# Recurrent layers: the pieces of one software-pipelined step in a new order on TensorE, ScalarE and VectorE

## What is computed

```python
xa = _ln(x, ln1_w, ln1_b)
sx = concatenate([state[:, 1:2] - xa[:, :1], xa[:, :-1] - xa[:, 1:]], axis=1)
xxx = tanh((xa + sx * maa_x) @ maa_w1).reshape(b, l, 5, DM)
xxx = einsum('blfd,fde->blfe', xxx, maa_w2)
xm = xa[:, :, None] + sx[:, :, None] * (maa_stack + xxx)
xk, xw, xv, xr, xg = (xm[:, :, j] for j in range(5))
w = exp(-exp(time_decay + tanh(xw @ td_w1) @ td_w2))
r, k, v, g = xr @ Wr.T, xk @ Wk.T, xv @ Wv.T, silu(xg @ Wg.T)
# over tokens, per head of 16 channels: out = r (u*k*v + s); s = k*v + w*s
og = group_norm(out) * gn_w + gn_b
x1 = x + og * g @ Wo.T
xc = _ln(x1, ln2_w, ln2_b)             # sx2: the shifted difference of xc
rr = sigmoid((xc + sx2 * ffn_maa_r) @ Wfr.T)
kk = square(relu((xc + sx2 * ffn_maa_k) @ Wfk.T))
return x1 + rr * (kk @ Wfv.T)
```

## Time and profile before

| | us |
|---|---|
| median of 3 runs | 3420.65 |
| lowest, highest | 3415.77, 3423.81 |
| the profiled execution, its own time | 3415.86 |
| its span, first to last instruction | 3414.1 |

### The profile page before, as it was taken

How to read it: one execution, slowest core, us unless ns; L and a number is a source line. 1 busy time by engine, 2 the same in 40 slices (tenths; PEclk the granted TensorE clock), 3 DMA queues, 4 the chain that set the end, 5 groups by cost and what they waited for, 6 DMA issues and landing times.

```text
span 3414.1 us, 77104 instructions
## 1 busy us (share of the span) xinstructions
PE 3145.0 (92%) x32684; PEld 2330.3 (68%) x32684; DVE 2327.4 (68%) x3819; ACT 1822.0 (53%) x3311; POOL 226.0 (7%) x457
## 2 busy tenths in 40 slices
PE   6789999999999999999999999999799899998998
PEld 4567777777777777776777777776566666665666
DVE  3667777777677767768777677776546667566566
ACT  3445555555554555555545555554446656556565
POOL 0000000000000000000000000000011010010110
PEclk8889999999999999999999999999999999999999
DMA  3223322343333233333323333323344224133221
GB/s 124 69 75 107 122 99 99 124 143 115 110 118 105 100 111 127 118 121 118 112 94 115 122 116 108 118 106 140 113 102 96 68 62 115 38 86 103 57 68 51
DMA packets 110357, 349.41 MB, mean 102 GB/s; under 512 B 22848, under 2 KB 56256, under 8 KB 84032
## 3 DMA queue, kind: packets, MB, share of 16 engines
q0 software_dynamic: 39936, 234.91, 21.1%
q1 hardware_dynamic: 69648, 106.28, 9.9%
q10 hardware_dynamic: 432, 3.28, 0.3%
HBM read 252.11 MB, written 16.78 MB: 79 GB/s over the span
## 4 chain that ended last, share of the span: by engine, by line
PE 77%; DVE 12%; ACT 6%; DMA 2%; issue 2%; SPq 1%; DVEq 0%; ACTq 0%
PE psum L742 34%; PE psum L751 6%; PE psum L909 4%; PE psum L927 3%; PE psum L879 3%; PE psum L808 3%; PE psum L869 3%; PE psum L792 3%; PE psum L899 2%; DMA rw<-rw 2%; DVE psum L1718 2%; PE psum L884 2%; ACT rw L1210 2%; PE psum L695 2%; PE psum L675 1%
## 5 line engine op out<-in xcount | busy, mean ns | idle before, releaser
L742 PE MATMUL psum<-rw 128*128 128x256 f32 x6144 | 1461.0, 396 | 73.0 <-DVE rw L1469 63.4
L742 PEld LDWEIGHTS psum<-rw 128*128 128x128 f32 x6144 | 1196.1, 198 | 292.3 <-DVE rw L1469 72.8
L1718 DVE CUSTOM_DVE_ANT_0 psum<-psum,mem 128x1024 f32<-128x1024 f32 x256 | 313.4, 1224 | 76.0 <-PE psum L899 75.8
L1274 ACT ACTIVATE rest<-psum,mem 128x1024 f32<-128x1024 f32 x256 | 284.8, 1113 | 90.4 <-DVE mem L1718 88.5
L909 PE MATMUL psum<-ident,rest 128*128 128x128 f32 x2048 | 269.6, 275 | 2.7 <-DVE mem L1677 1.5
L1514 DVE SCALAR_TENSOR_TENSOR rw<-psum,rw 128x256 f32<-128x256 f32 x480 | 196.1, 475 | 100.3 <-PE psum L708 60.0
L909 PEld LDWEIGHTS psum<-ident,rest 128*128 128x128 f32 x2048 | 234.5, 141 | 42.2 <-issue 14.6
L1143 ACT ACTIVATE rw<-psum 128x512 f32<-128x512 f32 x192 | 113.4, 603 | 272.0 <-PE psum L742 271.7
L1899 POOL DMA_DIRECT2D rw<-big_dram x192 | 101.2, 528 | 2367.7 <-PE psum L742 2333.8
L1186 ACT ACTIVATE rw<-psum,own 128x256 f32<-128x256 f32 x384 | 208.4, 714 | 84.5 <-PE psum L792 84.5
L751 PE MATMUL psum<-rw 128*128 128x512 f32 x432 | 222.1, 633 | 15.0 <-ACT rw L1147 7.9
(11 more groups left out here) (157 smaller groups left out, 4446.3 us busy)
## 6 DMA issues: line engine op xcount, KB each, us to landing
rw<-big_dram POOLq DMA_DIRECT2D x192, 1024.0 KB, 5.1
side<-mem POOLq DMA_DIRECT2D x256, 128.0 KB, 4.1
rw<-xs_dram SPq DMA_DIRECT2D x32, 512.0 KB, 3.4
side<-mem SPq DMA_DIRECT2D x256, 64.0 KB, 2.0
rw<-rw SPq DMA_DIRECT2D x192, 64.0 KB, 2.0
rw<-rw SPq DMA_DIRECT2D x384, 32.0 KB, 3.2
xs_dram<-rw SPq DMA_DIRECT2D x24, 512.0 KB, 2.9
rw<-x_dram SPq DMA_DIRECT2D x16, 512.0 KB, 3.5
```

The lines of the kernel that those rows point to most:

```text
L742: last = mm(t[:, o * TC:(o + 1) * TC], big[:, k, P * m:P * m + P], src[:, k, 0:TC], start=k == 0, stop=k == KT - 1, skip_group_check=True)
L1274: s_ring.empty(f(probs[:, n % HPT, :].rearrange("p (a s) -> p a s", a=2), s_ring.bank(n, "s"), ACT.Exp, scale=-1.0, bias=mx[:, n % 8:n % 8 ...
L1718: maxima.inc(nc.vector.tensor_tensor_reduce(t, t, mbias.rearrange("p (a s) -> p a s", a=2), 1.0, 3.4e38, ALU.add, ALU.min, accum_out=mx[:, ...
```

## The change

The tiles of the attention's first batch, which the last steps carry along (`batch_tile`, `after`, `centred`, `scaled`), are moved among them in the same manner. The core of the diff:

```diff
-C_TILES = [(2, "fr0", "act"), (2, "fr1", "act"), (2, "fk0", "act"), (1, "wo0", "dve"), (1, "wo1", "dve"), (2, "fk1", "act"), (2, "fv0",
-           "dve"), (2, "fv1", "dve"), (1, "s1", "act"), (1, "m1", "dve"), (1, "s2", "act"), (1, "i1", "dve")]
+C_TILES = [(2, "fr0", "act"), (2, "fr1", "act"), (2, "fk0", "act"), (1, "wo0", "dve"), (1, "wo1", "dve"), (2, "fk1", "act"), (1, "s1", "act"), (2, "fv0", "dve"), (2, "fv1", "dve"), (1, "m1", "dve"), (1, "s2", "act"), (1, "i1", "dve")]
...
# VectorE, in norm_c
-                if which == "mix":
+                if which == "mixr":
                     dve.wait_ge(c_dve.sem, c_dve.at(it, "sx"))
                     c_dve.inc(mixture(mixr, sxc, xa_c, lambda k: par(layer, FMR, k)), it, "mixr")
+                if which == "mixk":
+                    dve.wait_ge(c_dve.sem, c_dve.at(it, "sx"))
                     c_dve.inc(mixture(mixk, sxc, xa_c, lambda k: par(layer, FMK, k)), it, "mixk")
...
# VectorE, start of the step
+                if has_e:
+                    norm_c(e, "mixk")
+                if has_c:
+                    gated(c, 1)
                 if has_b:
                     level1(b)
-                    own_values(b)
...
# VectorE, end of the step
-                if has_c:
-                    norm_c(c, "mix")
-                if has_b:
-                    gated(b, 0)
-                    gated(b, 1)
+                if has_b:
+                    group_variance(b, 1)
                 if s == ITS - 1:
                     after(0, "q0")
                     scaled(0, 0)
+                if has_b:
+                    group_scale(b, 1)
+                if s == ITS - 1:
                     scaled(0, 1)
+                if has_b:
+                    gated(b, 0)
```

More of the change, by code:

```diff
@@ L113 @@
-B_TILES = [("P0a", "dve"), ("P0b", "dve"), ("P1", "dve"), ("P2a", "dve"), ("P2b", "dve"), ("VT0", "act"), ("VT1", "act"), ("KT0", "act"),
-           ("KT1", "act"), ("P4a", "dve"), ("P4b", "dve"), ("P4c", "dve"), ("P4d", "dve"), ("U00", "act"), ("U01", "act"), ("U02", "act"),
-           ("U03", "act"), ("U10", "act"), ("U11", "act"), ("U12", "act"), ("U13", "act")]
+A_TILES = [("s1", "act"), ("m1", "dve"), ("s2", "act"), ("i1", "dve"), ("w1", "act"), ("w2w0", "dve"), ("w2v0", "dve"), ("w2k0", "dve"), ("w2w1", "dve"), ("w2v1", "dve"), ("w2k1", "dve"), ("w1g", "act"), ("v0", "act"), ("td1", "act"), ("td2_0", "act"), ("td2_1", "act"), ("v1", "act"), ("w2r0", "dve"), ("w2g0", "dve"), ("w2r1", "dve"), ("w2g1", "dve"), ("k0", "act"), ("k1", "act"), ("r0", "act"), ("r1", "act"), ("g0", "act"), ("g1", "act")]
@@ L122 @@
 A_DVE = ["rc", "sx", "lm", "mix_w", "mix_v", "mix_k", "mix_r", "mix_g"]
 A_ACT = ["sq", "xa", "pad", "edge", "w"]
[L124 to L128, removed]
+LEAF_DVE = ["p0", "p1", "u1w", "u1r", "u1k", "p2a", "p2b", "u2w", "u2r", "u2k", "o1", "o2a", "p4a", "p4b", "p4c", "p4d", "u8", "u4r", "u4k", "o2b", "o4a", "o4b", "o4c", "o4d"]
@@ L1349, in _ @@
                     feed(e, "fk", 1)
+                if has_c:
+                    norm_c(c, "s1")
                 if has_b:
@@ L1355, in _ @@
                 if has_b:
-                    spread_queries(b)
+                    scan_inputs(b, 0)
+                if s == ITS:
+                    after(0, "v0")
+                if has_n:
+                    stream(n, "v", 0)
+                if has_b:
+                    update(b, 1, 0)
+                if has_n:
+                    decay_in(n)
+                if has_b:
                     carry(b, 0)
+                    update(b, 1, 1)
                     scan_inputs(b, 1)
                 if has_n:
-                    stream(n, "v", 0)
-                    decay_in(n)
+                    decay_out(n)
                 if has_c:
-                    norm_c(c, "s1")
-                if s == ITS:
-                    after(0, "v0")
-                if has_b:
-                    update(b, 1, 0)
-                    update(b, 1, 1)
+                    norm_c(c, "sq")
                 if has_n:
-                    decay_out(n)
+                    stream(n, "v", 1)
+                if has_c:
+                    norm_c(c, "s2")
                 if has_b:
@@ L1796, in _ @@
                     gather(b, "P4c", "o4c", 1, 4)
+                if s == ITS + 1:
+                    mask_bias(0)
                 if has_c:
                     residual(c, 1)
-                if has_b:
-                    gather(b, "P4d", "o4d", 0, 4)
                 if has_n:
@@ L1803, in _ @@
                     mixed(n, "w")
+                if s == ITS - 1:
+                    centred(0, 0)
+                if has_n:
+                    mixed(n, "v")
+                if has_b:
+                    gather(b, "P4d", "o4d", 0, 4)
+                if s == ITS - 1:
+                    centred(0, 1)
                 if has_b:
                     scan(b, 0)
-                if has_n:
-                    mixed(n, "v")
                 if has_e:
@@ L1840, in _ @@
                 if has_b:
+                    group_scale(b, 0)
+                if has_c:
+                    norm_c(c, "mixr")
+                if has_b:
                     group_mean(b, 1)
-                    group_scale(b, 0)
+                if s == ITS - 1:
+                    inverse(0)
+                if has_b:
                     group_variance(b, 1)
-                if has_c:
-                    norm_c(c, "sx")
+                if s == ITS - 1:
+                    after(0, "q0")
+                    scaled(0, 0)
                 if has_b:
```

163 lines of the change are left out of this document (82 added, 81 removed).

## The result

The changed kernel takes 3201.8 us (median of 4 runs, 3200.9 to 3203.9) against 3419.2 us for the kernel before on the same chip: a ratio of 0.9364, 95% interval 0.9348 to 0.9380. It is faster by 217 us. The forecast had the sign and the mechanism, but the time lies 61 us under it and 33 us under the low end of its range. Times in this document are medians of a kernel's four executions; of the last experiment's four, one of 10592 us is left out.

The account below looks back on a forecast made before the run. TensorE bounds the kernel. Waits 102, DMA 4, clock 48, less 10.5 for new waits, make 143.5 us; with first steps 8 and tail 3, 154.5 off 3415.9, plus 2 for the median: 3263 us, range 3235 to 3320.

Parts of the forecast that it names:

- the clock term: Slow clock in the 21 full steps: 48 of 54.7 us would go, bounds 0 and 54.7.
- Steps 1, 3, 4: TensorE's waits in full steps go: fr0 for mixr 60.5 us, lora_two for v1's copy 33.6, td2 for its tanh 7.9.
- Step 2: gated(c, 1) moved into the next step: s1 on ScalarE still comes 2 us before TensorE's m1 needs it.
- Step 5: TensorE's waits for v_m's DMAs: WV and WK loads start 0.6 us earlier; 4 us gain taken, bounds 0 to 10.4.
- Step 6: WV's load before v0: 1.4 us spare at the median landing; one at the maximum would cost 7 us, once.
- Step 7: TensorE's wait of P4a behind KT0, 7.2 us, and the remaining 6 us of waits stay.
- Steps 8 and 10: VectorE idles 3 us before scan0, later handovers hold by 0.9 to 6; P1's bank is free at 13.0, due 13.6.
- Step 9: VectorE's tail from lora_two(n, 1) on: scan1 ends 0.5 us before outputs need it, mixed r 0.3 before r0.
- B: Thin handovers slip 1.5 us a step more and half the clock loss stays: 3320 us, chance 0.14.
- C: TensorE's waits go but the clock still falls, by narrow matmuls or micro-idles: 3311 us, chance 0.08.
- D: SyncE's queue: load_own's DMAs come late for own_turned(0), delaying scan1 and outputs: slower, 3431 us, chance 0.03.
- E: fr0 and lora_two find another wait in place of the old: 3400 to 3425 us, chance 0.03.

Follow-up runs that it names:

- the last experiment: Changed kernel with scan_inputs(b, 0) back ahead of the first updates on ScalarE: 3201.0 us, ratio 0.9365.
- fv1 back: Changed kernel with fv1 back ahead of updates(1,0) on TensorE and v0 behind them: 3228.1 us.
- the two fillers: Changed kernel with two or four idle VectorE instructions ahead of scan1 in the full steps: 3218.0 us with two, 3242.0 with four.
- 1.8 us at fr0: Changed kernel with TensorE's fr0 also waiting for gated(c, 1) in the full steps: 3243.1 us.
- Both, and the middle: Kernel before with mixr/mixk moved, the second lora_two apart, s1 and v0 earlier, fv1 between td1 and td2, mixed v ahead of scan0: 3318.5 us.
- the first two edits: Kernel before with mixr behind sx and mixk at the next step's start (3344.1 us), or lora_two(n, 1) behind updates(1,1) and s2 (3371.6); together 3301.0.

## Why the prediction was right in kind and 61 us off in size

Two steps failed: the allowance of 10.5 us for handovers that slip, and the clock term, sized 48 us where 72.6 were measured. The step's floor had been worked out and was right: the new order laid end to end with the durations of the earlier trace rows closed at 90.3 us, and 90.15 were measured. The forecast went by 92.3. The misses, term by term:

| term | forecast | measured | difference |
|---|---|---|---|
| waits of the full steps, net | 95.5 | 116.5 | 21.0 |
| clock and busy time | 48 | 72.6 | 24.6 |
| first steps | 8 | 17.7 | 9.7 |
| tail | 3 | 7.1 | 4.1 |
| offset of the median | -2 | 0 | 2 |

- **Steps 1, 3, 4 right.** The 102 us of waits went, by the mechanisms named. Apart, the first is worth 77 us with its clock, the second 49.
- **Step 2 right.** g1's and s1's end on ScalarE hid behind P0; TensorE has no wait there. By itself, the drain that the Trainium skill (ScalarE: Activation LUTs, What ACT_TABLE_LOAD costs) adds to the load would have fitted too. The traces show the load's 1.28 us alone: in the kernel of "fv1 back" one load starts at 1312.70, as the instruction ahead of it ends, and the next starts at 1314.00.
- **Step 5 mis-sized.** 10.4 us, not 4. The mechanism that I gave for a gain was there, and I took the lesser end, though the 11 waits were 0.95 us in the mean and the loads' shift worked on every one of them.
- **Step 6 right.** Its handover of 1.4 us of spare slipped in one step of 21, for 1.42 us, when the load was issued 2.7 us late.
- **Step 7 wrong in part.** 7.2 us of P4a stayed; of the other 6.2 us only 2.1 did.
- **Steps 8 and 10 right.** VectorE idles before scan0 as marked, and TensorE doesn't see it:

```profile
DVE rw L1624 <- ACT rw L1176: 65.7, 21, 3.1
```

- **Step 9: the spare too small, the allowance wrong.** The marks gave 0.5 and 0.3 us; by the traces it is some 0.75. On top of that I charged 10.5 us for slips, reasoning that marks good to 0.3 us will sometimes miss. The marks did miss, to the safe side here, and none of the thin handovers of VectorE and ScalarE shows a wait over 0.2 us in any of the 21 steps. The only slip is WV's, 1.42 us in all. An allowance of 0.5 us a step described no event.
- **The clock: the term failed, twice.** First, the base. I took a step with a mean clock of 1.00 as TensorE's full-clock time, 90.56 us, though my own marks gave 90.3 for the whole step, waits included; so the clock's share came out as 54.7 us where half of the 122.9 us at 0.50 is 61.5. Then I held back 7 of it for causes not seen; all 61.5 went. The other 11.1 us are TensorE's own time by order, which no row of before shows; only the difference between the marks and the 90.56 hinted at it.
- **First steps mis-sized.** In them, too, the waits named go, and 17.7 us came within my bounds of 0 to 20; this was not taken apart by a run.
- **Rivals B and C.** B (handovers slip): only WV's did, once, and the two fillers show what it would look like: beyond the spare a delay costs an ordinary step its own length, with one fall or two in 21 steps and not half the clock loss. C (the clock falls anyway, by the narrow stretch or by micro-idles): the changed kernel runs through the same narrow stretch in 21 steps without a fall, and with P4a's wait of 0.34 us in each. By itself, the rule of the Trainium skill (TensorE: Matmul & The Clock Gate, A second HAM failure mode: psum-queue depth-cycling) has micro-idles between groups swing the clock; the traces agree for idles amid narrow matmuls, in most steps behind those of 1.5 and 1.6 us, with single falls behind one of 0.7, two of 1.1 and one of 1.4 us, and not for the 0.3 to 0.5 us that come in every step, nor for 1.3 us ahead of the outputs, 19 times without a fall.
- **Rivals D and E.** D (SyncE's queue): VectorE's wait for load_own's DMAs, 112.2 us in all before, is gone from its list after. But it came closer than the 5 us of room that I gave it. In the kernels with two and four fillers and with 1.8 us at fr0, which have the changed order, these DMAs land 11.7 to 17.6 us after the first issue where I had 12.7 to 13.2, and own_turned(0) starts at 17.84 at the earliest: 0.2 us of room at the least. WR's load starts 10.2 us after the first of them there; with fv1 back it starts at 4.4, and they land at 11.8 to 13.5. In "Both, and the middle" D's mechanism is what costs. E: no other wait took the place.
- **The range.** Its low end, 3235, is worked out as it was said to be: 3263 less 10.5 (all margins holding), 6.7 (the clock loss wholly gone) and 12 (the full bound of the first steps) is 3234. It leaves out the bounds listed for the DMA waits (6.4) and the tail (7) and the 2 us of the offset; with these it is some 3218. A further 18 us are missing in the clock term: its bound of 54.7 lay 6.8 under the 61.5 that the falls cost, and TensorE's own 11.1 was in no term.

## What to carry to other kernels

Where an engine is bound and its waits repeat in every step, lay the new order end to end: if every handover has room, the step's floor is the forecast, and a discount for slips needs a handover that is named and late. A removed wait is worth its length plus half the clock's fall behind it, and whether there is one is read from the record behind that very wait, not from its length. The room at a handover is read in a step where the reader does wait, not from the total time, which other steps blur. Moving a matmul also moves the weight load that follows it: look at which small DMAs it then runs beside, and what on the engine that needs them stands behind. The middle of this order cost 17 us on top of the first two edits because of that; the rest of the order as a whole, which has the same middle, brought 99.

## What the runs showed of the hardware

- The granted clock's fall behind a wait depends on its place as well as its length: 16 of 21 behind 1.5 us amid narrow matmuls, 2 of 21 behind 1.8 us between full-width projections; there 12 of 21 at 2.9 us (in the kernel before), and 18 of 21 at 3.4.
- Where TensorE waits for VectorE's scan, its matmuls start 0.1 us behind the end of the scan's row.
- TensorE's busy time for the same 21,840 matmuls at full clock was 1882 to 1891 us in the new order and the kernels made from it, and 1894 to 1905 in the old and the kernels made from that.
- The second pair of v_m's DMAs (4 of 64 KB), beside the loads of two weights, took 7.1 to 10.7 us from first issue to last landing, and with these loads started 0.6 us earlier against them 6.3 to 8.9; the longest of either is the one step in which the loads came late.
- 16 DMAs of 32 KB, issued over some 11 us, landed 11.8 to 14.5 us after the first issue where a weight's load started 4.4 or 5.4 us after it, and 11.7 to 17.7 where it started 10.2 us or more after it.
